# A four-block transformer kernel: SiLU from exponential and logarithm in chunks, and GpSimd's layer norms and bias sum spread over slots

## The chip, the cores and the metric

One core of a Trainium2 chip runs the program. The metric is the device time of one execution, in microseconds (us); lower is better. The kernel is written as five instruction queues, one for each engine: PE (TensorE, matrix products), DVE (VectorE), ACT (ScalarE), POOL (GpSimd) and SP (SyncE, which issues all transfers). Each queue runs in its own order, and the queues meet only at semaphores.

## The reference

The input x is 8 batches of 512 tokens of width 128. Four blocks follow each other, each on the layer norm of x and added to x:

```
x = x + attn_a(layernorm(x))     # 16 heads of width 8, causal, ALiBi slope 1, biases
x = x + ffn(layernorm(x))
x = x + attn_b(layernorm(x))     # full 512x512 scores -> importance of tokens -> 51 picked keys
                                 # + 64 compressed keys; attention over those 115
x = x + ffn(layernorm(x))

ffn(x):  gate = x @ wg.T ; up = x @ wu.T          # wg, wu: 384 x 128, dequantised from int
         return (silu(gate) * up) @ wd.T          # silu(g) = g * sigmoid(g)
layernorm(x) = (x - mean) / sqrt(var + 1e-5)
```

Everything is float32; scores use stacks of bfloat16 parts that together carry float32.

## The kernel before, in words

The work of a batch is written as a list of **slots**. In each slot every engine does the few instructions that it has there, and then goes to the next slot. The counter of a batch is called `a` in the code (its own slots run from -44 to 246), and batch b starts 64 slots after batch b-1, so that four to five batches are in work at once. Slots have no fixed length: a slot is as long as the slowest queue makes it. There are 739 slots in all.

What lies where in a batch's own count:
- -41 to -30: first layer norm, q, k and v of attention A (the P_ constants, lines 423 to 430).
- 0 to 24: first pass over the causal scores, two score tiles a slot, from which VectorE takes the row maxima (`causal_scores` line 1153, `causal_maxima` line 912). 32 to 56: second pass, where ScalarE takes exponentials (line 798) and TensorE weighs the values (`weigh`, line 1189).
- 61 to 74: output projection, residual, layer norm, and the first feed-forward block. I call it **block A**: A_GATE 66, 67, 68; A_SILU 69; A_UP 70, 71, 72; A_DOWN 74.
- 75 to 84: layer norm and projections of attention B. 96 to 160: its **main tiles**, one 128x512 tile of scores a slot.
- 164 to 224: choosing tokens, attention over 115 keys. 226 to 245: projection, residual, layer norm, and the second feed-forward block, **block S**: S_GATE 235, 236, 237; S_SILU 238; S_UP 240, 241, 242; S_DOWN 243.

Modulo 64, block A of batch b lies beside the first causal pass of batch b+1 (slots 2 to 10 of it), and block S of batch b beside the second causal pass of batch b+3 (slots 43 to 51 of it). Both lie beside main tiles of attention B of some batch, except at the ends of the program.

A main tile goes through four engines: TensorE writes its scores into one of three banks (line 1223, one slot ahead); VectorE takes the maximum of each row (`nmB`, line 1045); ScalarE the exponential (line 811) and the logarithm of the sum (line 814); GpSimd a threshold (`thr`, line 680); VectorE, one slot later and at the end of its slot, an entropy sum (`entropy`, line 951, instruction at line 955), which frees the bank.

The order of VectorE in a slot g is: maximum of main tile g; the causal row maxima of the two score tiles that TensorE made in slot g-1; the batch's own steps, among them `hidden` (line 946); the entropy sum of main tile g-1. The order of TensorE in a slot is: scores of main tile g+1; own steps, among them `into_seven` (line 1269), which makes the gate and up products; column sums (`influence`); causal scores. The order of ScalarE is: exponentials of the causal tiles (second pass); main tile; own steps. GpSimd: `thr` of main tile g, then own steps.

The feed-forward block has three chunks c of 128 hidden rows. All products of it, gate and up, go through one bank, bank 7, and `claim` (line 1134) makes TensorE wait until the last user of the bank has been read. Before the change ScalarE copies each gate chunk out in the same slot (line 840, helper line 727). In slot SILU ScalarE runs Silu over all three chunks at once, 128x1536 (line 785), which stands between two loads of the function table (one is recorded at line 785, one at line 786), as all its other functions are in one other table. VectorE multiplies each up chunk from bank 7 by the gate in the slot after it was made (`hidden`). So from `up` to `hidden` to the next `up` TensorE and VectorE take turns.

GpSimd's layer norm `ln` (line 641) does in one slot: variance plus epsilon, the power -1/2, and four 128x128 normalisations (line 652). It lies one slot after VectorE's statistics; TensorE transposes the result (line 1144) two slots later. The sum of x and the output bias, four additions of 128x128 (line 704), lies in slot XBO = 19.

## Time and profile before

| | |
|---|---|
| three timed runs | 1942.92, 1942.50, 1940.46 us; median 1942.5 us |
| the profiled execution | 1941.34 us |
| its span | 1939.2 us, 26667 instructions |
| mean granted clock of TensorE | 0.687 of full speed |
| busy | PE 1524.0 us (79%), DVE 1224.2 us (63%), ACT 1006.8 us (52%), POOL 385.6 us (20%) |
| main tiles | maxima from 245.3 to 1789.5 us of the span, one of 512 in each slot |

The span is that of the profiled execution, and 2.1 us of its time lie around it. A share of busy time is a mean over the program. What sets the length of a slot is found by looking at the instructions of that slot: which queue has no idle time in it, and for whom the others wait. The start of the `nmB` maximum (line 1045) is used as the mark of a slot, since there is just one in each.

### The profile page before, as it was taken

How to read it: one execution, taken by the hardware profiler on the slowest of the kernel's cores; microseconds unless marked ns; L12 is line 12 of the kernel's file. 1: busy time of each engine (PE TensorE's matmuls, PEld its weight loads, DVE VectorE, ACT ScalarE, POOL GpSimd, SP SyncE). 2: the span in 40 equal slices, each digit the busy share in tenths (PEclk: the TensorE clock that was granted, in tenths of full speed). 3: DMA queues.
4: the chain of work that ended last, by engine and by line, in shares of the span. 5: the costliest groups of instructions: out<-in, count | busy, mean ns of one | idle time of the engine just before them, and what ended most of it. 6: DMA issues, size and time to landing. Idle time of an engine off the chain costs nothing.

```text
span 1939.2 us, 26667 instructions
## 1 busy us (share of the span) xinstructions
PE 1524.0 (79%) x8717; PEld 690.2 (36%) x8717; DVE 1224.2 (63%) x3259; ACT 1006.8 (52%) x2542; POOL 385.6 (20%) x900
## 2 busy tenths in 40 slices
PE   1687787878788888898889888788888878678655
PEld 1333443343344343353334343344334332321312
DVE  1503568866976577756876587757786667787211
ACT  1052276466556655656556655665565757546122
POOL 3110311320133011410133022310221012110100
PEclk9555588667766677668667786777666867665555
DMA  2110111121012110112012110221011002100000
GB/s 59 31 36 17 44 52 17 37 60 23 19 41 60 23 22 14 47 44 44 3 49 52 23 24 12 73 36 27 13 35 34 12 8 49 28 13 12 15 10 6
DMA packets 65626, 59.28 MB, mean 31 GB/s; under 512 B 11936, under 2 KB 63184, under 8 KB 65488
## 3 DMA queue, kind: packets, MB, share of 16 engines
q1 hardware_dynamic: 65488, 57.58, 13.3%
q8 instruction: 69, 1.13, 0.3%
q14 instruction: 69, 0.57, 0.1%
HBM read 39.10 MB, written 18.27 MB: 30 GB/s over the span
## 4 chain that ended last, share of the span: by engine, by line
PE 50%; DVE 23%; ACT 13%; issue 6%; POOL 5%; DMA 1%; ACTq 0%; SPq 0%; POOLq 0%; DVEq 0%
PE bank L1231 7%; PE bank L1271 7%; DVE nm L916 6%; DVE junk L955 5%; ACT setup L811 4%; PE bank L1223 4%; PE bank L1199 3%; PE bank L1254 3%; PE bank L1181 3%; PE bank L1159 3%; ACT pT L798 3%; DVE nmB L1045 3%; POOL xn L652 3%; DVE nm L923 2%; PE bank L1390 2%
## 5 line engine op out<-in xcount | busy, mean ns | idle before, releaser
L811 ACT ACTIVATE setup<-bank,nmB 128x512 f32<-128x512 f32 x512 | 350.3, 684 | 291.7 <-DVE nmB L1045 291.6
L955 DVE SCALAR_TENSOR_TENSOR junk<-bank,thr,setup 128x512 f32<-128x512 f32 x512 | 379.4, 741 | 84.8 <-POOL thr L680 81.5
L1045 DVE TENSOR_REDUCE nmB<-bank 128x1 f32<-128x512 f32 x512 | 351.2, 686 | 97.5 <-PE bank L1223 97.0
L1223 PE MATMUL bank<-k_stacks,q_stacks 48*128 48x512 bf16 x512 | 248.6, 487 | 135.5 <-DVE junk L955 133.1
L680 POOL TENSOR_TENSOR thr<-lnZ,nmB 128x1 f32<-128x1 f32 x512 | 96.5, 189 | 1223.5 <-ACT lnZ L814 1223.2
L916 DVE TENSOR_REDUCE nm<-bank 128x1 f32<-128x512 f32 (+3 forms) x512 | 223.7, 483 | 141.4 <-PE bank L1164 138.8
L798 ACT ACTIVATE pT<-bank 128x512 f32<-128x512 f32 (+1 forms) x384 | 184.1, 520 | 174.4 <-PE bank L1185 172.1
L1159 PE MATMUL bank<-k_stacks,q_stacks 52*128 52x512 bf16 (+3 forms) x512 | 177.1, 393 | 38.7 <-DMA k_stacks<-part_dram 17.7
L1231 PE MATMUL bank<-setup,rz 128*1 128x512 f32 x1024 | 196.6, 852 | 0.0
L1181 PE MATMUL bank<-q_stacks,k_stacks 55*128 55x384 bf16 (+3 forms) x512 | 159.2, 359 | 38.3 <-ACT pT L798 32.8
L1223 PEld LDWEIGHTS bank<-k_stacks,q_stacks 48*128 48x128 bf16 x512 | 49.5, 97 | 321.7 <-DVE junk L955 247.4
L1159 PEld LDWEIGHTS bank<-k_stacks,q_stacks 52*128 52x128 bf16 x512 | 54.5, 107 | 189.0 <-issue 121.8
L893 ACT ACTIVATE p<-bank 115x512 f32<-115x512 f32 x128 | 75.3, 588 | 87.3 <-PE bank L1390 87.0
L1199 PE MATMUL bank<-pT,vA 128*9 128x512 f32 (+3 forms) x1024 | 115.0, 554 | 1.0 <-ACT pT L798 1.0
L1162 PE MATMUL bank<-maskr,maskw 64*128 64x64 bf16 x512 | 114.6, 232 | 0.0
L1390 PE MATMUL bank<-s_stacks,kcst 51*115 51x512 bf16 x128 | 75.5, 590 | 49.4 <-ACT p L893 19.5
L814 ACT ACTIVATE lnZ<-Z 128x1 f32<-128x1 f32 x512 | 103.9, 203 | 16.2
L1164 PE MATMUL bank<-maskr,maskw 64*128 64x64 bf16 x512 | 109.0, 219 | 0.0
L1271 PE MATMUL bank<-xnT,wuT 128*128 128x512 f32 x96 | 81.8, 947 | 31.6 <-DVE gated L949 30.3
L1181 PEld LDWEIGHTS bank<-q_stacks,k_stacks 55*128 55x128 bf16 x512 | 52.7, 103 | 145.4 <-issue 81.5
L1183 PE MATMUL bank<-maskr,maskw 64*128 64x64 bf16 x512 | 104.2, 218 | 0.0
L811 ACT ACTIVATION_READ_ACCUMULATOR setup<-bank,nmB 128x1 f32 x512 | 102.2, 200 | 0.0
(193 smaller groups left out, 2437.4 us busy)
## 6 DMA issues: line engine op xcount, KB each, us to landing
part_dram<-part SPq DMA_DIRECT2D x16, 768.0 KB, 3.2
q_stacks<-part_dram SPq DMA_DIRECT2D x192, 64.0 KB
k_stacks<-part_dram SPq DMA_DIRECT2D x192, 64.0 KB
s_stacks<-part_dram SPq DMA_DIRECT2D x48, 128.0 KB
x<-in_L_attn_a_x_dram SPq DMA_DIRECT2D x8, 256.0 KB, 3.2
x_dram<-x SPq DMA_DIRECT2D x8, 256.0 KB, 2.2
x<-x_dram SPq DMA_DIRECT2D x8, 256.0 KB, 2.9
out_dram<-x SPq DMA_DIRECT2D x8, 256.0 KB, 2.2
```

Of the source, the lines that this page charges most:

```text
L798: act.activation(pT[h % HPQ][:, c * T:c * T + WIDTH[c]], bank[3 + u % 2][:, 0:WIDTH[c]], ACT.Exp).then_inc(s_free[3 + u % 2], 1)
L811: act.activation(E[:, n % NE, :], RING[n % RN][:, :], ACT.Exp, bias=nmB[mb % 2][:, h, t:t + 1], accum_out=Z[mb % 2][:, h, t:t + 1]).then_i ...
L916: last = dve.tensor_reduce(nm[0][:, t, h:h + 1], bank[k][:, at:at + (t + 1) * P], AX_X, ALU.max, negate=True)
L955: dve.scalar_tensor_tensor(out=junk[:, :], in0=RING[n % RN][:, :], scalar=thr[mb % 2][:, h, t:t + 1], in1=E[:, n % NE, :], op0=ALU.max, op ...
L1045: dve.tensor_reduce(nmB[mb % 2][:, h, t:t + 1], RING[n % RN][:, :], AX_X, ALU.max, negate=True).then_inc(s_bm, 1)
L1159: pe.matmul(bank[k][:, at:at + (t + 1) * P], qst[0][0:A_SC, h, t * P:(t + 1) * P], kst[0][0:A_SC, h, 0:(t + 1) * P], start=True, stop=True)
L1162: pe.matmul(bank[k][:, at + t * P:at + t * P + HF], maskw[:, 2, :], maskr[:, 2, :], start=False, stop=True, skip_group_check=True)
L1181: pe.matmul(bank[k][:, at:at + w], kst[0][0:A_MX, h, j * P:(j + 1) * P], qst[0][0:A_MX, h, j * P:T], start=True, stop=True)
L1199: last = pe.matmul(bank[5][QROWS * j:QROWS * j + HD + 1, k * P:T], vA[:, k, HPQ * g + j, :], pT[j][:, c * T + at:c * T + at + T - k * P], ...
L1223: pe.matmul(RING[n % RN][:, :], qst[1][0:B_SC, h, t * P:(t + 1) * P], kst[1][0:B_SC, h, :], start=True, stop=True).then_inc(s_bs, 1)
L1231: last = pe.matmul(INFL[QROWS * t:QROWS * t + 1, :], rz[mb % 2][:, h, t:t + 1], E[:, (NT * h + t) % NE, :], start=(h == 0), stop=(h == H - 1))
L1271: pe.matmul(bank[7][:, :], w, xnT[u][:, :], start=True, stop=True).then_inc(s_full[7], 1)
```

## The change

Two edits. First, Silu is replaced. VectorE takes each gate chunk out of bank 7, one slot after it was made, with a maximum against -85 (`gate`). ScalarE makes exp(-g) of it two slots after (`minus_gate`), and three slots after ln(1 + exp(-g)) and exp(-that), which is sigmoid(g) (`sigmoid`), in a new buffer `sigm`. GpSimd multiplies gate and sigmoid four slots after. Exponential and logarithm share one table, so no table is loaded. `hidden` then waits for its own chunk only. Second, GpSimd's layer norm is cut in three: the inverse root in the slot of the statistics, and two normalisations in each of the next two slots; the bias sum is cut into two slots.

```diff
@@ gpsimd
-                def ln(u, b):
+                def inverse_root(u, b):
                     pool.wait_ge(s_mv[u], b + 1)
                     pool.tensor_tensor(ve[u][:, :], mv[u][:, :, 1], eps[:, :], ALU.add).then_inc(s_ve[u], 1)
                     pool.wait_ge(s_ve[u], b + 1)
                     pool.tensor_tensor(rstd[u][:, :], ve[u][:, :], neghalf[:, :], ALU.pow).then_inc(s_rs[u], 1)
+
+                def normalise(u, b, half):
                     pool.wait_ge(s_rs[u], b + 1)
...
-                    for t in range(NT):
+                    for t in (2 * half, 2 * half + 1):
...
-                            if a == LN_AT[u]:
-                                ln(u, b)
+                            if a == STATS[u]:
+                                inverse_root(u, b)
+                            for half in range(2):
+                                if a == STATS[u] + 1 + half:
+                                    normalise(u, b, half)
...
+                        for k in range(2):
+                            for c in range(FC):
+                                if a == GATE[k][c] + 4:
+                                    pool.wait_ge(s_sg[k], FC * b + c + 1)
+                                    pool.wait_ge(s_free[7], turn[7]["gate", k, c, b] + 1)
+                                    pool.tensor_tensor(gated[:, c, :], gated[:, c, :], sigm[:, c, :], ALU.mult
+                                                       ).then_inc(s_sil[k], 1)
+                        for half in range(2):
+                            if a == XBO + half:
...
@@ scalar
-                def silu(k, b):
-                    act.wait_ge(s_free[7], turn[7]["gate", k, FC - 1, b] + 1)
-                    act.activation(gated[:, :, :], gated[:, :, :], ACT.Silu).then_inc(s_sil[k], 1)
-                    act.preload_act_table_set("natural_log_exp_and_others")
+                def minus_gate(k, c, b):
+                    act.wait_ge(s_free[7], turn[7]["gate", k, c, b] + 1)
+                    act.activation(sigm[:, c, :], gated[:, c, :], ACT.Exp, scale=-1.0).then_inc(s_eg[k], 1)
+
+                def sigmoid(k, c, b):
+
+                    act.wait_ge(s_eg[k], FC * b + c + 1)
+                    act.activation(sigm[:, c, :], sigm[:, c, :], ACT.Ln, bias=onesf[:, 0:1]).then_inc(s_lg[k], 1)
+                    act.wait_ge(s_lg[k], FC * b + c + 1)
+                    act.activation(sigm[:, c, :], sigm[:, c, :], ACT.Exp, scale=-1.0).then_inc(s_sg[k], 1)
...
-                                if a == GATE[k][c]:
-                                    out_of(7, ("gate", k, c, b), gated[:, c, :], bank[7][:, :])
-                            if a == SILU[k]:
-                                silu(k, b)
+                                if a == GATE[k][c] + 2:
+                                    minus_gate(k, c, b)
+                                if a == GATE[k][c] + 3:
+                                    sigmoid(k, c, b)
@@ vector
-                    dve.wait_ge(s_sil[k], b + 1)
+                    dve.wait_ge(s_sil[k], FC * b + c + 1)
...
+                def gate(k, c, b):
+
+                    dve.wait_ge(s_full[7], turn[7]["gate", k, c, b] + 1)
+                    dve.tensor_scalar(gated[:, c, :], bank[7][:, :], -85.0, None, ALU.max).then_inc(s_free[7], 1)
...
+                                if a == GATE[k][c] + 1:
+                                    gate(k, c, b)
                                 if a == UP[k][c] + 1:
                                     hidden(k, c, b)
@@ tensor
-                    pe.wait_ge(s_xn[u], b + 1)
+                    pe.wait_ge(s_xn[u], 2 * (b + 1))
```

The waits for `s_xbo` count two steps a batch instead of one. Nothing else changes.

## Rows read from the trace of the kernel before

**Rows 1.** The page's chain of waits that ended last, shares of the span by engine.
```profile
PE 50%; DVE 23%; ACT 13%; issue 6%; POOL 5%; DMA 1%; ACTq 0%; SPq 0%; POOLq 0%; DVEq 0%
```
**Rows 2.** Groups of instructions by line: busy us, mean ns, idle before and its releaser.
```profile
L955 DVE SCALAR_TENSOR_TENSOR junk<-bank,thr,setup 128x512 f32<-128x512 f32 x512 | 379.4, 741 | 84.8 <-POOL thr L680 81.5 <-issue 0.5
...
L652 POOL TENSOR_SCALAR xn<-x,mv,rstd 128x128 f32<-128x128 f32 x128 | 100.8, 799 | 3.3
...
L658 POOL TENSOR_TENSOR rest<-qf,part 128x512 f32<-128x512 f32 x32 | 37.0, 1157 | 20.8 <-ACT part L753 20.8
...
L949 DVE TENSOR_TENSOR gated<-bank,gated 128x512 f32<-128x512 f32 x48 | 32.8, 682 | 50.1 <-ACT gated L785 30.2 <-PE bank L1271 19.9
...
L727 ACT ACTIVATE gated<-bank 128x512 f32<-128x512 f32 x48 | 28.3, 589 | 44.4 <-PE bank L1271 44.4
...
L785 ACT ACTIVATE gated<-gated 128x1536 f32<-128x1536 f32 x16 | 23.7, 1482 | 0.2
...
L785 ACT ACT_TABLE_LOAD x16 | 20.5, 1283 | 0.3
...
L757 ACT ACTIVATE part<-rest 128x512 bf16<-128x512 f32 x32 | 19.8, 620 | 1.5 <-POOL rest L658 1.5
```
**Rows 3.** Three stretches: length; busy PE, PEld, DVE, ACT, POOL; PE clock; DMA share; GB/s.
```profile
946.08:953.14 7.06, 6.43 (x45) 2.48 (x43) 7.06 (x21) 4.74 (x13) 1.66 (x4) 1.00 0.06 14
955.40:967.39 11.99, 8.64 (x34) 2.31 (x32) 9.21 (x22) 6.35 (x16) 0.76 (x4) 0.62 0.01 3
...
885.77:891.86 6.09, 2.38 (x14) 1.31 (x15) 1.54 (x5) 6.02 (x11) 0.19 (x1) 0.85 0.30 44
```
**Rows 4.** Timeline of VectorE, block A of batch 4: start us, length us, what, idle before.
```profile
955.40 0.68 DVE L1045 TENSOR_REDUCE nmB<-bank 128x1 f32<-128x512 f32 x1
...
958.83 0.69 DVE L1045 TENSOR_REDUCE nmB<-bank 128x1 f32<-128x512 f32 x1
960.32 1.23 DVE L916 TENSOR_REDUCE nm<-bank 128x1 f32<-128x256 f32 x2 [0.80 <-PE bank L1164]
...
962.79 0.69 DVE L1045 TENSOR_REDUCE nmB<-bank 128x1 f32<-128x512 f32 x1
...
967.39 0.68 DVE L1045 TENSOR_REDUCE nmB<-bank 128x1 f32<-128x512 f32 x1
```
**Rows 5.** Timeline of TensorE in the same block: a gate product and two up products.
```profile
946.53 1.12 PE L1271 MATMUL bank<-xnT,wgT 128*128 128x512 f32 x2
...
957.99 1.86 PE L1271 MATMUL bank<-xnT,wuT 128*128 128x512 f32 x2 [2.07 <-DVE gated L949]
...
962.26 2.08 PE L1271 MATMUL bank<-xnT,wuT 128*128 128x512 f32 x2 [1.18 <-DVE gated L949]
```
**Rows 6.** Timeline of ScalarE around the SiLU of block S, batch 1.
```profile
882.74 1.09 ACT L798 ACTIVATE pT<-bank 128x512 f32<-128x512 f32 x2 [0.57 <-PE bank L1185]
...
884.74 1.28 ACT L785 ACT_TABLE_LOAD   x1
...
888.83 1.08 ACT L798 ACTIVATE pT<-bank 128x512 f32<-128x512 f32 x2
...
893.48 0.70 ACT L798 ACTIVATE pT<-bank 128x256 f32<-128x256 f32 x2 [0.79 <-PE bank L1185]
```
**Rows 7.** Timeline of TensorE around the same SiLU.
```profile
889.48 0.33 PE L1181 MATMUL bank<-q_stacks,k_stacks 55*128 55x384 bf16 x1 [3.80 <-ACT pT L798]
...
895.99 1.52 PE L1271 MATMUL bank<-xnT,wuT 128*128 128x512 f32 x2
```
**Rows 8.** Timeline of TensorE, block A of batch 0, before the first main tile.
```profile
187.35 2.07 PE L1271 MATMUL bank<-xnT,wuT 128*128 128x512 f32 x2 [1.45 <-DVE gated L949]
```
**Rows 9.** Timeline of VectorE, block A of batch 7, with no causal pass beside it.
```profile
1584.53 0.75 DVE L955 SCALAR_TENSOR_TENSOR junk<-bank,thr,setup 128x512 f32<-128x512 f32 x1 [1.90 <-POOL thr L680]
```
**Rows 10.** Timeline of VectorE, block S of batch 7, at the end of the program.
```profile
1924.95 0.69 DVE L949 TENSOR_TENSOR gated<-bank,gated 128x512 f32<-128x512 f32 x1 [17.66 <-ACT gated L785]
```
**Rows 11.** Who waited for the layer norm's output xn: us in total, times.
```profile
  PE bank L1144: 44.1, 18
```

More of the change, by code:

```diff
@@ L132, in hybrid_block @@
         gated = sb("gated", [P, FC, T])
+        sigm = sb("sigm", [P, FC, T])
         ktok = [sb(f"ktok{s}", [P, 2, NT, P]) for s in range(2)]
@@ L229, in hybrid_block @@
         s_rzo = [sem(f"sums_inverted{s}") for s in range(2)]
+        s_eg = [sem(f"gate_exponentials{s}") for s in range(2)]
+        s_lg = [sem(f"gate_logarithms{s}") for s in range(2)]
+        s_sg = [sem(f"gate_sigmoids{s}") for s in range(2)]
         s_sil = [sem(f"silu_done{s}") for s in range(2)]
@@ L447, in hybrid_block @@
         F_STATS = 75
-        F_LN = 76
         F_LNT = 78
@@ L481, in hybrid_block @@
         SLOTS = FIRST + NMAIN * (B - 1) + S_STORE + 2
-        GATE, SILU, UP, DOWN = (A_GATE, S_GATE), (A_SILU, S_SILU), (A_UP, S_UP), (A_DOWN, S_DOWN)
-        STATS, LN_AT, LN_TURN = (P_STATS, A_PROJ + 1, F_STATS, S_PROJ + 1), (P_LN, A_LN, F_LN, S_LN), (
-            P_TURN, A_LNT, F_LNT, S_LNT)
+        GATE, UP, DOWN = (A_GATE, S_GATE), (A_UP, S_UP), (A_DOWN, S_DOWN)
+        STATS, LN_TURN = (P_STATS, A_PROJ + 1, F_STATS, S_PROJ + 1), (P_TURN, A_LNT, F_LNT, S_LNT)
         LN_BANK = (4, 7, 7, 7)
@@ L578, in _ @@
                             if b:
-                                sp.wait_ge(s_xbo, b)
+                                sp.wait_ge(s_xbo, 2 * b)
                             sp.dma_start(xs0[:, :, :], x[b].rearrange("(t p) d -> p t d", p=P)).then_inc(s_xin, DMA)
@@ L645, in ln @@
                     pool.tensor_tensor(rstd[u][:, :], ve[u][:, :], neghalf[:, :], ALU.pow).then_inc(s_rs[u], 1)
+                def normalise(u, b, half):
                     pool.wait_ge(s_rs[u], b + 1)
-                    if (u, b) in norm_before:
+                    if half == 0 and (u, b) in norm_before:
                         v, other = norm_before[u, b]
                         pool.wait_ge(s_full[LN_BANK[v]], turn[LN_BANK[v]]["ln", v, other] + 1)
-                    for t in range(NT):
+                    for t in (2 * half, 2 * half + 1):
                         last = pool.tensor_scalar(xn[:, t, :], xs[u][:, t, :], mv[u][:, t, 0:1], rstd[u][:, t:t + 1],
@@ L698, in _ @@
                                                    ALU.mult).then_inc(s_sq, 1)
-                        if a == XBO:
-                            pool.wait_ge(s_xin, DMA * (b + 1))
-                            if b:
-                                pool.wait_ge(s_x2st, DMA * b)
-                            for t in range(NT):
-                                last = pool.tensor_tensor(xs1[:, t, :], xs0[:, t, :], bo[:, :], ALU.add)
-                            last.then_inc(s_xbo, 1)
+                        for k in range(2):
[7 more added lines that the diff above has]
+                            if a == XBO + half:
+                                if half == 0:
+                                    pool.wait_ge(s_xin, DMA * (b + 1))
+                                    if b:
+                                        pool.wait_ge(s_x2st, DMA * b)
+                                for t in (2 * half, 2 * half + 1):
+                                    last = pool.tensor_tensor(xs1[:, t, :], xs0[:, t, :], bo[:, :], ALU.add)
+                                last.then_inc(s_xbo, 1)
                         if a == A_TMAX + 1:
@@ L1065, in _ @@
                         if a == A_PROJ + 1:
-                            dve.wait_ge(s_xbo, b + 1)
+                            dve.wait_ge(s_xbo, 2 * (b + 1))
                             residual(xs1, ("proj", 0, b))
```

5 lines of the change are left out of this document (removed).

## The prediction

> **What bounds the kernel now.** I read the shares of busy time first, and they settle nothing: no engine is full over the span. The chain that ended last [rows 1] passes from TensorE to VectorE to ScalarE and has only 5% on GpSimd: a kernel of stages with different limits. So I looked at the slots that the change touches, one block A and one block S, and asked in each which queue has no idle time. In block A, the three slots behind the gate products last 7.06 us together and VectorE is busy for 7.06 us of them (first row of [rows 3]): VectorE is the limit there, TensorE runs beside it at its full clock (1.00, 2.4 GHz), and ScalarE has 2.3 us to spare. In block S of batch 1 the stretch with the SiLU is 6.09 us long; ScalarE is busy 6.02 us of it, TensorE 2.38 us (third row of [rows 3]). There ScalarE is the limit. The same instruction, taken out, is worth different things in the two places.
>
> **The cost of the SiLU now.** A table load takes 1.28 us, the Silu over 128x1536 1.48 us [rows 2], and there are two loads: 4.05 us by the durations, 4.09 us from the first load to the next exponential (888.83 - 884.74, [rows 6]). Over 16 blocks that is 65 us of ScalarE, but only what someone waits for counts. The Trainium skill's page ScalarE: Activation LUTs (section What ACT_TABLE_LOAD costs) says that a switch costs about 2.66 us, a drain of 1.38 us being added to the load. By that each block would give back some 2.7 us more, estimated from the page, and the sum below, with five exposed blocks, would be 14 us lower. In the rows the next instruction follows the load at once, so the measured 4.09 us stands.
>
> **Block S, batches 0 to 4** (second causal pass and main tiles beside it). Removed: the 4.09 us and three copies of 0.59 us [rows 2], 5.9 us of ScalarE. Added: nine passes over 128x512; the nearest row is a conversion from SBUF to SBUF of that size, 0.62 us (line 757, [rows 2]); nine make 5.6 us. So ScalarE does nearly as much as before, only in smaller pieces: 0.6 us in slot 237, 1.9 us in 238 and 239, 1.2 us in 240. Each of these slots also has two causal exponentials (1.09 us [rows 6]) and a main tile, together 2.0 us from 882.74 to 884.74. From 882.74, three slots then take 3.9 + 3.9 + 3.2 = 11.0 us, and the causal exponentials of the slot behind them would start at 893.8 instead of 893.48 [rows 6]. ScalarE as such gains nothing. What is gained is on TensorE: it idled 3.80 us in one piece [rows 7], and its second up product came at 895.99 [rows 7]. With the causal exponentials of each slot no longer behind one long block, I place that product between 892.6 and 894.7, depending on whether TensorE is at its full or half clock: 1.3 to 3.3 us earlier. I take 2, times 5: **-10 us**; bounds 0 (ScalarE full) and -3.8 each. Block S of batch 5 has no causal pass and gains 0.5; in the last two, with nothing beside, `hidden` waited for the Silu until 1924.95 [rows 10], while the first chunk would be ready before its up product; the copy by VectorE costs 0.1 more than ScalarE's, so 0.3 each. Together **-11 us**.
>
> VectorE's copy in block S is covered: VectorE idles most of those slots (busy 1.54 of 6.09 us [rows 3]). Behind it waits the entropy sum, late by up to 0.7 us, which frees a score bank that TensorE wants a slot later; I count nothing.
>
> **Block A, batches 1 to 6** (first causal pass and main tiles beside it). The Silu is hidden here: the up products wait for `hidden` [rows 5], and of the 30.2 us for which `hidden` ever waited for a Silu [rows 2], 17.66 lie in the very last block [rows 10]. So nothing comes back. What is added lies on the full engine: three copies out of bank 7 on VectorE. The nearest row is `hidden`, the same size out of the same bank: 0.68 us, some 0.60 when the next one overlaps it [rows 2]. And the copy brings a new wait. ScalarE emptied bank 7 in the slot in which TensorE filled it; VectorE does it one slot later, behind its main maximum and its causal maxima. TensorE's queue has the next gate product in front of the causal scores of that slot, so it stops at `claim` until VectorE is through, and VectorE then waits for causal scores that come after the product. This turn-taking is in the trace already, in the up slots: TensorE waits 2.07 and 1.18 us for `hidden` [rows 5], the causal maxima wait 0.80 us for TensorE [rows 4], and the slots behind the up products last 3.43, 3.96 and 4.60 us (starts 955.40, 958.83, 962.79, 967.39 [rows 4]), where those behind the gate products last 7.06 / 3 = 2.35 us. The granted clock falls as well, from 1.00 to 0.62 over that stretch [rows 3], so a product takes 2.08 us (1.2 GHz) instead of 1.12 us (2.4 GHz) [rows 5].
> With the change the first gate slot only gets the copy, 2.35 + 0.60 = 2.95 us; the second and third are built like the second and third up slot, 3.96 and 4.60 us. Sum 11.5 us against 7.06: +4.4 us a block, times 6: **+26 us**. Bounds: 3 x 0.60 = 1.8 us if TensorE were never late, 7 us if in addition the half clock stretches the two slots behind by a product's excess of 1 us each. A value near the up slots is right because the code is the same, step for step.
>
> **Block A of batch 0** has no main tiles beside it. TensorE waits 1.45 us in the up slots [rows 8]; twice that for the second and third gate product: **+3 us**. **Block A of batch 7** has no causal pass. There Silu is exposed: the entropy sum waits 1.90 us for a threshold that is late behind it [rows 9]. Spread over slots most of that goes, less the new copies: **-1 us**, bounds -3 and +1.
>
> **GpSimd.** The multiplication costs 1.16 us a chunk (nearest row, line 658, two inputs of 128x512 [rows 2]); 48 of them are 56 us of an engine that is 20% busy. Each stands behind the threshold of its slot and before the next one, in slots of 2.3 us and more; nothing on the path. In block A `hidden` follows only one slot later: threshold, then 1.16 us, and by my count the first chunk is ready 0.2 us before VectorE gets to it. Were it late, some tenths a block would be added, inside the bounds. If that cover were gone, the price would be 1.16 us a block in A. The root now waits for VectorE's statistics in their own slot; behind it on GpSimd stands only the threshold of the next slot, which needs a later maximum of VectorE. The split of the layer norm takes a piece of 4 x 0.80 = 3.2 us (line 652, [rows 2]) plus 1.2 us for the root off the way of thresholds. VectorE's waits for thresholds sum to 81.5 us [rows 2], but nearly all of it is the plain latency through ScalarE. The other place is TensorE's wait for xn, 44.1 us in 18 pieces [rows 11], most of it in the start and the end, where the chain root, four normalisations, transposition is as long as before. I take **-2 us** for both, bounds 0 and -5. The bias sum ends a slot later. Its readers are the residual 42 slots on, and on SP's queue the load of the next x, which so starts about a slot later (2.35 us by the slots above, more in others) and is wanted three slots after that: 0. No transfer is added, and what stands behind that load on SP is issued two slots on.
>
> **Sum.** 26 + 3 - 1 - 11 - 2 = +15 us on the profiled execution's 1941.3 us: 1956.3 us. The median of the three runs is 1.2 us above that execution, so I say 1957 us.
>
> **Rivals.**
> *The gain in block S outweighs (faster).* Place: the 3.80 us idle of TensorE in five blocks S, and the half clock after it (0.85 over that stretch [rows 3]). If all of the 3.8 us came back, 19 us, plus the exposed Silu of batch 7 (3 us) and 5 us from the layer norm, against turn-taking at full clock in block A, 3 us x 6 = 18 and 2 for batch 0: -7 us, 1935. It decides if block A costs under 2.5 us each. For it: ScalarE is plainly the limit in the row of 6.09 us. Against: ScalarE's work there shrinks by 0.3 us only. Chance 0.17.
> *A draw.* The same terms in the middle, block A at 2.5 and block S at -3: 1942 us. Chance 0.10.
> *The half clock spreads.* TensorE idles in the gate slots, its granted clock falls to 1.2 GHz there and stays so up to the up products: 7 us a block in A, nothing gained in S: 42 + 3 - 2 = +43, 1985 us. For it: the clock of 0.62 in the up slots. Chance 0.13.
> That the second edit does nothing (all layer-norm slots as long as before) is possible in each of these cases and moves the time by 2 us only. My forecast has the remaining 0.60.
>
> **How the numbers follow.** About 0.2% (4 us) is about what a measurement of this kernel can tell from no change. Slower by more than that: 0.60 + 0.13 = 0.73; within it: 0.10; faster: 0.17. The range goes from 1936 (the faster rival without its last microseconds) to 1978 (the bounds of block A without the worst).
>
> **What would show it.** Right: slots behind the gate products in blocks A of 1 to 6 grow from 7.06 us to 10 to 12 us, with TensorE idle before the second and third gate product, released by VectorE's copy; the stretch of block S around the old Silu has no TensorE idle piece over 2 us and the second up product comes earlier; ScalarE's nine passes take 0.6 us each; no table load but the first. Wrong: gate slots in block A under 9 us, or blocks S shorter by more than 3 us each, or layer-norm slots that shorten by over 1 us in every period.

## The result, and the profile after

| | before | after |
|---|---|---|
| median of four runs each, same chip | 1942.0 us (1940.5 to 1942.9) | 1967.0 us (1963.2 to 1970.2) |
| the profiled execution, its span | 1941.3, 1939.2 us | 1970.2, 1968.5 us |
| mean granted clock | 0.687 | 0.669 |

The ratio is 1.0125, 95% interval 1.0098 to 1.0153: slower by 25 us. In a second comparison (`e8_after_again`, below) it is 1.0149.

The page of after, shares of busy time, and the chain that ended last by engine:
```profile
PE 1549.8 (79%) x8717; PEld 697.8 (35%) x8717; DVE 1255.9 (64%) x3307; ACT 1002.5 (51%) x2590; POOL 446.9 (23%) x948
...
PE 53%; DVE 24%; ACT 10%; issue 7%; POOL 4%; DMA 1%; SPq 0%; ACTq 0%; DVEq 0%; POOLq 0%
```
VectorE has 32 us more to do, GpSimd 61, ScalarE 4 less. In the chain [rows 1] ScalarE's share went from 13% to 10% and TensorE's from 50% to 53%: the program waits less for ScalarE, and more for TensorE.

Groups by line of after (columns as in [rows 2]; L971 is VectorE's new copy, L966 `hidden`, L796, L801 and L803 the three passes, L706 GpSimd's product, L368 the only table load):
```profile
L1295 PE MATMUL bank<-xnT,wgT 128*128 128x512 f32 x96 | 81.1, 939 | 29.1 <-DVE gated L971 27.8 <-ACT xnT L738 0.7 <-DVE vcat L1033 0.6
L1295 PE MATMUL bank<-xnT,wuT 128*128 128x512 f32 x96 | 79.6, 923 | 31.0 <-DVE gated L966 29.3 <-DVE gated L971 1.6
...
L706 POOL TENSOR_TENSOR gated<-gated,sigm 128x512 f32<-128x512 f32 x48 | 60.9, 1269 | 29.6 <-ACT sigm L803 29.6
...
L801 ACT ACTIVATE sigm<-sigm,onesf 128x512 f32<-128x512 f32 x48 | 34.0, 708 | 0.3
L971 DVE TENSOR_SCALAR gated<-bank 128x512 f32<-128x512 f32 x48 | 32.8, 683 | 28.7 <-PE bank L1295 28.6
L966 DVE TENSOR_TENSOR gated<-bank,gated 128x512 f32<-128x512 f32 x48 | 32.8, 682 | 24.9 <-PE bank L1295 22.7 <-POOL gated L706 2.2
L803 ACT ACTIVATE sigm<-sigm 128x512 f32<-128x512 f32 x48 | 30.2, 630 | 1.5
L796 ACT ACTIVATE sigm<-gated 128x512 f32<-128x512 f32 x48 | 29.6, 616 | 18.4 <-DVE gated L971 18.4
...
L368 ACT ACT_TABLE_LOAD x1 | 1.3, 1283 | 0.8 <-PEq L1458 0.8
```
The gate product of before:
```profile
L1271 PE MATMUL bank<-xnT,wgT 128*128 128x512 f32 x96 | 66.7, 782 | 6.3 <-ACT gated L727 5.0 <-ACT xnT L727 0.7 <-DVE vcat L1011 0.6
```
Its idle time rose from 6.3 to 29.1 us, and VectorE's copy ends nearly all of it. Its mean duration rose from 782 to 939 ns: more of the gate products run at TensorE's lower clock. They now look like the up products beside them (923 ns, 31.0 us).

**Block A of batch 4, the gate slots.** Stretches of after, columns as in [rows 3]; the first is the three slots behind the gate products, the second the four behind them, with the up products:
```profile
961.88:974.02 12.14, 8.83 (x39) 2.77 (x38) 9.17 (x22) 5.22 (x13) 1.67 (x4) 0.58 0.04 9
...
974.02:987.18 13.16, 9.74 (x53) 3.32 (x51) 11.29 (x28) 7.90 (x19) 4.42 (x7) 0.76 0.01 1
```
7.06 us at full clock with a full VectorE [rows 3] became 12.14 us at 0.58, with VectorE idle for 3 us. The timelines of TensorE and VectorE in after:
```profile
960.50 1.12 PE L1295 MATMUL bank<-xnT,wgT 128*128 128x512 f32 x2
964.21 2.07 PE L1295 MATMUL bank<-xnT,wgT 128*128 128x512 f32 x2 [1.80 <-DVE gated L971]
969.08 2.07 PE L1295 MATMUL bank<-xnT,wgT 128*128 128x512 f32 x2 [1.51 <-DVE gated L971]
```
```profile
961.88 0.69 DVE L1067 TENSOR_REDUCE nmB<-bank 128x1 f32<-128x512 f32 x1
962.48 1.07 DVE L933 TENSOR_REDUCE nm<-bank 128x1 f32<-128x128 f32 x3
963.48 0.68 DVE L971 TENSOR_SCALAR gated<-bank 128x512 f32<-128x512 f32 x1
...
964.74 0.68 DVE L1067 TENSOR_REDUCE nmB<-bank 128x1 f32<-128x512 f32 x1
966.96 1.40 DVE L933 TENSOR_REDUCE nm<-bank 128x1 f32<-128x512 f32 x3 [1.54 <-PE bank L1188]
...
968.36 0.66 DVE L971 TENSOR_SCALAR gated<-bank 128x512 f32<-128x512 f32 x1
```
TensorE's first product is ready at 961.6; VectorE does its main and causal maxima first and copies at 963.48; the second product starts at 964.21, at the lower clock; the causal scores come behind it, so VectorE's next causal maxima wait 1.54 us. In the slot behind, the same happens again (TensorE waits 1.51 us for the copy).

**Block S of batch 1.** ScalarE in after, around the sigmoid passes, and the stretch that answers to the 6.09 us of [rows 3]:
```profile
903.27 0.69 ACT L828 ACTIVATE setup<-bank,nmB 128x512 f32<-128x512 f32 x1
...
904.20 0.71 ACT L801 ACTIVATE sigm<-sigm,onesf 128x512 f32<-128x512 f32 x1
904.93 0.63 ACT L803 ACTIVATE sigm<-sigm 128x512 f32<-128x512 f32 x1
905.47 0.61 ACT L796 ACTIVATE sigm<-gated 128x512 f32<-128x512 f32 x1
905.99 1.06 ACT L815 ACTIVATE pT<-bank 128x512 f32<-128x512 f32 x2
```
```profile
905.34:909.01 3.67, 2.14 (x15) 0.95 (x15) 1.54 (x7) 3.61 (x9) 0.97 (x2) 1.00 0.22 50
```
The slot went from 6.09 to 3.67 us, and ScalarE still fills it (3.61 us). TensorE's longest idle piece there is 1.37 us, where 3.80 stood [rows 7]. The second up product of this block in after:
```profile
913.57 2.07 PE L1295 MATMUL bank<-xnT,wuT 128*128 128x512 f32 x2
```
Counted from the start of slot 46 (899.84 us in after, 880.27 us in before) it comes after 13.73 us, where it came after 15.72 us (895.99 [rows 7]).

**The whole program by stretches.** I subtracted the starts of the main maxima (line 1045, after line 1067) between two traces, slot by slot, and summed over the 8 periods. Differences to the profiled execution of before, in us; slots modulo 64. "S gate" are slots 41 to 47, "S SiLU" 48 to 50, "behind S" 51 to 57, "tail" is from the last main tile on:

| | start | A gate (3 to 5) | rest of A | S gate | S SiLU | behind S | other | tail | sum |
|---|---|---|---|---|---|---|---|---|---|
| after | 2.1 | 31.5 | -0.8 | 9.4 | -13.7 | 0.2 | -1.2 | 1.8 | 29.3 |
| e8_after_again | 0.9 | 30.3 | -0.5 | 6.9 | -13.7 | 2.6 | -5.2 | 0.2 | 21.5 |
| e1_act_copy | 0.4 | 0.0 | -0.3 | 4.5 | -12.3 | 2.5 | -6.2 | 1.3 | -10.3 |
| e12_copy_s | -0.9 | 0.2 | 0.0 | 9.6 | -13.3 | 2.7 | -6.2 | -0.3 | -8.2 |
| e13_copy_a | 1.9 | 30.5 | 5.2 | 12.0 | -13.1 | -0.3 | 1.3 | 1.5 | 38.9 |
| e4_copy_first | 1.2 | 11.4 | 5.7 | 5.3 | -14.5 | 2.6 | -3.6 | 0.5 | 8.6 |
| e9_norms_whole | -1.7 | 2.2 | 1.5 | -3.6 | -13.1 | -0.2 | 10.8 | 1.2 | -3.0 |
| e2_norms_only | 0.0 | 0.5 | 1.4 | 7.8 | -5.3 | -2.5 | -5.0 | 0.0 | -3.0 |
| e5_no_silu | -2.4 | 0.5 | -3.2 | -7.8 | -41.0 | 1.9 | 1.5 | -0.7 | -51.2 |
| e7_one_pass | -0.3 | 2.4 | -0.3 | 3.4 | -35.5 | 0.1 | -0.5 | -0.8 | -31.6 |
| e6_early_s | 0.0 | 0.5 | -0.3 | 32.2 | -28.1 | 2.5 | 0.6 | 1.6 | 8.9 |
| e10_spread_s | -1.7 | 0.1 | -0.8 | 13.9 | -34.4 | 37.0 | -0.2 | 6.9 | 20.8 |
| e11_up_late | -0.5 | 0.1 | -0.6 | 8.5 | -18.3 | 25.8 | -2.0 | 0.2 | 13.1 |

Each row is one execution. "A gate" and "S SiLU" repeat within 1.2 us in the two executions of after; "S gate" and "other" differ there by 2.5 and 4.0 us; for the 2.5 the section on the hardware shows the reason. Terms of that size in one trace are not read as effects of an edit.

### The profile page after: what moved, and what is told of

Read it like the earlier page. It is cut to its first block, busy times and chain, and to the rows that moved or that the text cites. A ratio compares the mean times of both kernels' runs of the same rounds, so it can differ in the third digit from the quotient of the medians.

```text
span 1968.5 us, 26859 instructions
## 1 busy us (share of the span) xinstructions
PE 1549.8 (79%) x8717; PEld 697.8 (35%) x8717; DVE 1255.9 (64%) x3307; ACT 1002.5 (51%) x2590; POOL 446.9 (23%) x948
## 4 chain that ended last, share of the span: by engine, by line
PE 53%; DVE 24%; ACT 10%; issue 7%; POOL 4%; DMA 1%; SPq 0%; ACTq 0%; DVEq 0%; POOLq 0%
PE bank L1295 8%; PE bank L1255 8%; DVE nm L933 5%; DVE junk L977 5%; PE bank L1247 4%; PE bank L1223 4%; PE bank L1183 3%; PE bank L1278 3%; PE bank L1205 3%; ACT setup L828 3%; DVE nmB L1067 3%; ACT pT L815 3%; DVE nm L940 3%; PE bank L1414 2%; PE bank L1238 2%
## 5 line engine op out<-in xcount | busy, mean ns | idle before, releaser
L1183 PE MATMUL bank<-k_stacks,q_stacks 52*128 52x512 bf16 (+3 forms) x512 | 185.7, 409 | 37.7 <-DMA k_stacks<-part_dram 17.3
L1255 PE MATMUL bank<-setup,rz 128*1 128x512 f32 x1024 | 205.3, 888 | 0.0
L1186 PE MATMUL bank<-maskr,maskw 64*128 64x64 bf16 x512 | 118.7, 239 | 0.0
L1188 PE MATMUL bank<-maskr,maskw 64*128 64x64 bf16 x512 | 112.4, 224 | 0.0
L1295 PE MATMUL bank<-xnT,wuT 128*128 128x512 f32 x96 | 79.6, 923 | 31.0 <-DVE gated L966 29.3
L1295 PE MATMUL bank<-xnT,wgT 128*128 128x512 f32 x96 | 81.1, 939 | 29.1 <-DVE gated L971 27.8
L1207 PE MATMUL bank<-maskr,maskw 64*128 64x64 bf16 x512 | 103.6, 218 | 0.0
```

Source lines behind the costliest of these rows:

```text
L1183: pe.matmul(bank[k][:, at:at + (t + 1) * P], qst[0][0:A_SC, h, t * P:(t + 1) * P], kst[0][0:A_SC, h, 0:(t + 1) * P], start=True, stop=True)
L1186: pe.matmul(bank[k][:, at + t * P:at + t * P + HF], maskw[:, 2, :], maskr[:, 2, :], start=False, stop=True, skip_group_check=True)
L1255: last = pe.matmul(INFL[QROWS * t:QROWS * t + 1, :], rz[mb % 2][:, h, t:t + 1], E[:, (NT * h + t) % NE, :], start=(h == 0), stop=(h == H - 1))
L1295: pe.matmul(bank[7][:, :], w, xnT[u][:, :], start=True, stop=True).then_inc(s_full[7], 1)
```

## The experiments

Ratios are to the kernel before on the same chip, with the 95% interval. All but `e2_norms_only` and `e5_no_silu` start from after.

**Who copies.** `e1_act_copy` gives the copy back to ScalarE, in the slot of the product:
```diff
@@ scalar, after's kernel
+                                if a == GATE[k][c]:
+                                    out_of(7, ("gate", k, c, b), gated[:, c, :], bank[7][:, :])
@@ vector
-                                if a == GATE[k][c] + 1:
-                                    gate(k, c, b)
```


> The changed kernel, but ScalarE copies each gate chunk out of bank 7 in the slot in which TensorE made it, as before the change; VectorE's copy is gone, everything else of the change stays (no clamp at -85, which these inputs do not need). Theory A (the loss is the turn-taking of TensorE and VectorE at bank 7): the three slots behind the gate products in blocks A fall from 12.1 us back to 7.1 us (31 us over the program), batch 0 gives back 2 us more, the gate slots of blocks S 2 us each, and the 2.4 us gained at the old Silu in each block S stay: about 1925 us, 0.99 of the kernel before. Theory B (the loss comes from GpSimd's multiplication, the later `hidden`, or ScalarE's nine passes): the gate slots fall but the slots of the up products grow, and the time stays over 1955 us.

Measured: 1935.5 us, ratio 0.9984 (0.9971 to 0.9997). The gate slots of block A are as before (0.0 in the table), so VectorE's copy is the whole of their 31 us, and not the product on GpSimd or the smaller passes: theory A holds there. The rest of the change is worth 3 us in this form, well below the 14 us that theory A expected of it.

`e8_after_again` is after, unchanged.

> The changed kernel again, on this chip beside the others, so that e1 and e4 can be held against it: all theories expect 1960 to 1970 us, 1.010 to 1.015 of the kernel before.

Measured: 1963.4 us, ratio 1.0149 (1.0104 to 1.0194).

**Order or length.** `e4_copy_first` keeps the copy on VectorE but places it ahead of the causal maxima:
```diff
@@ vector, after's kernel: behind the main maximum
+                        for k in range(2):
+                            for c in range(FC):
+                                if a == GATE[k][c] + 1:
+                                    gate(k, c, b)
+                    for b, a in now:
...
-                                if a == GATE[k][c] + 1:
-                                    gate(k, c, b)
```


> The changed kernel with one thing moved: VectorE's copy of the gate chunk stands in front of its causal row maxima, behind its main maximum, in the same slot. Theory A (TensorE waits for the copy, which waits behind the maxima): TensorE's idle pieces before the second and third gate product shrink from some 2 us to under 1, and the three slots of blocks A go from 12.1 us to 9 us, so about 1948 us in all. Theory B (it is VectorE's 0.6 us of added work and the half clock, not the order): slots stay at 11.5 us or more, 1963 to 1967 us.

Measured: 1944.5 us, ratio 1.0033 (1.0021 to 1.0046), near theory A's 1948. The gate slots of block A in batch 4, and TensorE's waits there:
```profile
947.27:956.12 8.85, 6.49 (x45) 2.45 (x43) 8.85 (x24) 4.50 (x12) 1.67 (x4) 1.00 0.06 13
```
```profile
948.61 1.12 PE L1298 MATMUL bank<-xnT,wgT 128*128 128x512 f32 x2 [0.81 <-DVE gated L971]
951.47 1.12 PE L1298 MATMUL bank<-xnT,wgT 128*128 128x512 f32 x2 [0.81 <-DVE gated L971]
```
8.85 us with VectorE busy for all of it, at full clock: 7.06 plus three copies of 0.60. TensorE still waits 0.81 us for each copy, but VectorE never waits for TensorE, so only the length counts. Of the 5.1 us of after's gate slots 1.8 are length, and 3.3 are order, the lower clock among them.

**Splitting the copy by block.** `e12_copy_s` keeps VectorE's copy in block S alone, `e13_copy_a` in block A alone (the condition is `k == 0` in the second kernel's vector part, with ScalarE's copy under `k == 1`, and the other way round in the first):
```diff
@@ e12_copy_s, from after's kernel
+                                if k == 0 and a == GATE[k][c]:
+                                    out_of(7, ("gate", k, c, b), gated[:, c, :], bank[7][:, :])
...
-                                if a == GATE[k][c] + 1:
+                                if k == 1 and a == GATE[k][c] + 1:
                                     gate(k, c, b)
```


> After, but ScalarE copies the gate chunks out of bank 7 in block A as before; only block S keeps VectorE's copy. This prices the term that the prediction counted as nothing. Theory that the copy in block S is covered: the time of e1_act_copy, ratio 0.998 to 0.999. Theory that it costs about 0.4 us a block by its length and up to 6 us over all through slots 42 to 45 (the difference of after and e1_act_copy there in the profiled executions): ratio 1.000 to 1.002. In both theories the three slots behind the gate products of block A stay at 7.06 us.

> The complement: after, but ScalarE copies the gate chunks in block S as before; only block A keeps VectorE's copy. If the two copies add up, e12_copy_s and e13_copy_a lie above e1_act_copy by parts that sum to the 1.5% between e1_act_copy and after. Theory that block A is all of it: ratio 1.013 to 1.015, as after. Theory that block S has a share of 6 us: ratio 1.009 to 1.012. The three slots behind the gate products of block A take about 12 us as in after.

Measured: `e12_copy_s` 1928.9 us, ratio 0.9947 (0.9933 to 0.9960); `e13_copy_a` 1979.8 us, ratio 1.0196 (1.0174 to 1.0217). Both theories of the first expectation missed: VectorE's copy in block S is neither free nor a cost, it gains 0.4% against `e1_act_copy`, and 0.5% to 0.7% if after and its repeat are held against `e13_copy_a`. So `e12_copy_s` is the fastest version here that still computes the SiLU, 10 us faster than before. The copy in block A costs more than either theory of the second expectation said: 2.1% of time (`e13_copy_a` against `e1_act_copy`), or 1.8% (after against `e12_copy_s`): 35 to 41 us. The two parts, -0.4% and +2.1%, add up to the 1.4% to 1.7% between `e1_act_copy` and after. The table finds 31 us of block A's loss in the three gate slots. For block S's gain I looked at the last two blocks S, which stand in the tail. `hidden` in `e1_act_copy`, then in `e12_copy_s`:
```profile
L968 DVE TENSOR_TENSOR gated<-bank,gated 128x512 f32<-128x512 f32 x48 | 32.8, 682 | 49.3 <-POOL gated L706 31.2 <-PE bank L1295 18.0
```
```profile
L968 DVE TENSOR_TENSOR gated<-bank,gated 128x512 f32<-128x512 f32 x48 | 32.8, 683 | 25.5 <-PE bank L1297 23.3 <-POOL gated L706 2.2
```
With ScalarE copying, its queue has the third copy ahead of the first chunk's logarithm and second exponential, and `hidden` waits for the product on GpSimd; with VectorE copying it doesn't. But 28.7 of the 31.2 us stand in the last two blocks S, where VectorE has little else to do, and most of that wait is idle time that costs nothing. From the first gate product of batch 7 to its second up product `e12_copy_s` takes 11.44 us and `e1_act_copy` 11.70: 0.26 us are gained. Of the 1.6 us by which the table's tail is shorter, 1.0 lies ahead of the first gate product of batch 6, where after and its repeat differ by 0.8 as well. So no trace shows where the 7 us between these two kernels lie: their profiled executions differ by 2 us in the other direction, each being off its median (1930.6 against 1935.5 us, and 1932.7 against 1928.9 us). The runs of `e12_copy_s` had a mean granted clock of 0.687 to 0.692, those of `e1_act_copy` 0.683 to 0.690, so TensorE's clock is a rival to the copy itself that I can't exclude.

**What the SiLU holds.** `e5_no_silu` is before with no SiLU and no table loads; the product with up uses the gate as it is:
```diff
@@ scalar, before's kernel
-                    act.activation(gated[:, :, :], gated[:, :, :], ACT.Silu).then_inc(s_sil[k], 1)
-                    act.preload_act_table_set("natural_log_exp_and_others")
+                    act.activation(gated[:, :, 0:1], gated[:, :, 0:1], ACT.Copy).then_inc(s_sil[k], 1)
```


> The kernel before without Silu and without its two table loads (the gate goes into the product as it is; a copy of three columns keeps the semaphore). It prices the Silu block: what can be won at most by taking it away. Theory A: nothing in blocks A 1 to 6, 3 us in block A of batch 7, 3.5 us in each of six blocks S: 1918 us. Theory B (it is exposed in every block): 16 times 4 us, 1880 us. Theory C (ScalarE's other work fills the place): under 2.4 us a block S, over 1925 us.

Measured: 1898.6 us, ratio 0.9806 (0.9756 to 0.9856). It lies between theory A (1918) and theory B (1880): the blocks S give back nearly 7 us each in the table, twice what A said. `e7_one_pass` is `e1_act_copy` without the logarithm and the second exponential; the gate is multiplied by exp(-g):
```diff
@@ scalar, e1_act_copy's kernel
-                    act.activation(sigm[:, c, :], sigm[:, c, :], ACT.Ln, bias=onesf[:, 0:1]).then_inc(s_lg[k], 1)
-                    act.wait_ge(s_lg[k], FC * b + c + 1)
-                    act.activation(sigm[:, c, :], sigm[:, c, :], ACT.Exp, scale=-1.0).then_inc(s_sg[k], 1)
+                    act.activation(sigm[:, c, 0:1], sigm[:, c, 0:1], ACT.Copy).then_inc(s_sg[k], 1)
```


> The kernel e1_act_copy without the logarithm and the second exponential (a copy of one column keeps the semaphore; GpSimd still multiplies), so the gate is multiplied by exp(-g) and not by the sigmoid. Theory A (six passes of 0.6 us in ScalarE's full slots of block S are what keeps the gain at 2 us): the slot that held the Silu is 4 us shorter than before, the one behind it 2.4 us, as without Silu at all: about 1905 us. Theory B (it is GpSimd or the up products): unchanged from e1, 1935 us.

Measured: 1910.1 us, ratio 0.9829 (0.9795 to 0.9863), as theory A said within 5 us. The slot of the SiLU in block S of batch 1, in `e5_no_silu` and in `e7_one_pass`:
```profile
870.10:872.07 1.97, 1.97 (x16) 0.85 (x14) 1.54 (x7) 1.94 (x7) 0.19 (x1) 1.00 0.14 45
```
```profile
876.00:878.48 2.48, 2.14 (x15) 0.95 (x15) 1.54 (x5) 2.45 (x9) 0.97 (x2) 1.00 0.13 38
```
6.09 us [rows 3], 3.67 in after, 2.48 with one pass of three, 1.97 with none. ScalarE is busy for all but 0.06 us of each: this slot is as long as ScalarE's work in it, and in `e5_no_silu` TensorE is full too. The whole SiLU is worth 38 us by the timed runs (1.94% of 1938.5); in the traces its slots in block S shrink by 41.0 us. The change got 13.7 of these back, `e7_one_pass` 35.5. So the passes hold the rest, and GpSimd's product, which `e7_one_pass` keeps, holds next to nothing.

**Can the passes be moved?** `e6_early_s` takes exp(-g) of block S straight from bank 7 in the slot of the product, and the other two passes one slot after it; ScalarE's copy of a chunk stands behind that exponential:
```diff
@@ scalar, e1_act_copy's kernel, block S (k = 1)
+                    act.activation(sigm[:, c, :], bank[7][:, :] if k else gated[:, c, :], ACT.Exp, scale=-1.0
...
-                                if a == GATE[k][c] + 2:
+                                if a == GATE[k][c] + 2 * (1 - k):
...
-                                if a == GATE[k][c] + 3:
+                                if a == GATE[k][c] + 3 - 2 * k:
```


> The kernel e1_act_copy (ScalarE copies the gate in its own slot) with the passes of blocks S moved two slots forward: exp(-g) straight from bank 7 in the slot of the product, logarithm and second exponential one slot later. Same number of passes, but most of them in slots where TensorE is the limit (ScalarE was idle half of them). Theory A (what the Silu cost in blocks S comes back only as far as ScalarE's passes leave the slots of the second causal pass that ScalarE limits): the two slots around the old Silu, which e1 shortened by 2.0 us a block, shorten by some 5 us, the gate slots grow by under 1 us: 10 to 15 us less than e1, 0.990 to 0.993 of the kernel before. Theory B (the rest of the 6.5 us belongs to GpSimd's multiplication or the clock): as e1, 0.998.

Measured: 1949.6 us, ratio 1.0049 (1.0029 to 1.0069), a miss. The SiLU slots gained 28 us, but the gate slots lost 32. Gate products of `e1_act_copy`, then of `e6_early_s`:
```profile
L1295 PE MATMUL bank<-xnT,wgT 128*128 128x512 f32 x96 | 68.5, 801 | 6.5 <-ACT gated L738 5.0 <-ACT xnT L738 0.7 <-DVE vcat L1035 0.6
```
```profile
L1299 PE MATMUL bank<-xnT,wgT 128*128 128x512 f32 x96 | 75.6, 879 | 11.8 <-ACT gated L738 10.3 <-ACT xnT L738 0.7 <-DVE vcat L1039 0.6
```
ScalarE's copy of the next chunk now stands behind the passes, TensorE waits 5.3 us more for it, and its products are slower (879 against 801 ns, 7.1 us in all). These are 12 of the 28 us by which the gate slots grew against `e1_act_copy`; the rest I did not trace.

`e11_up_late` moves the up and down products of block S and its store five slots later, `e10_spread_s` does so too and gives each pass a slot of its own:
```diff
@@ constants, e1_act_copy's kernel (both)
-        S_UP = (240, 241, 242)
-        S_DOWN = 243
-        S_STORE = 245
+        S_UP = (245, 246, 247)
+        S_DOWN = 248
+        S_STORE = 250
@@ e10_spread_s alone: logarithm, second exponential, GpSimd's product
+                                if a == GATE[k][c] + (3, 5)[k]:
+                                    log_of(k, c, b)
+                                if a == GATE[k][c] + (3, 8)[k]:
...
+                                if a == GATE[k][c] + (4, 9)[k]:
```


> The kernel e1_act_copy with blocks S stretched: up products, down product and store five slots later (S_UP 245 to 247), and ScalarE's nine passes one a slot (exponentials in slots 237 to 239, logarithms 240 to 242, second exponentials 243 to 245, GpSimd's products one slot after each). Theory A (three passes in one slot, 1.9 us, are more than the slot has left beside 2.0 us of other work; one pass, 0.6 us, is not): the slots 46 to 50 (modulo 64) shrink as without Silu, 4 us at 48 and 1 to 2 us at 49, and slots 51 to 56 grow by the up products moved there: 10 to 15 us less than e1, about 0.992 of the kernel before. Theory B (ScalarE's work is on the path whatever its place): as e1, 0.998.

> The kernel e1_act_copy with up products, down product and store of blocks S five slots later, but the passes three a slot as in e1: the control for e10. Theory A: the move itself gives nothing, 0.997 to 1.000 of the kernel before. Theory B (the place of the up products is what counts): the same as e10.

Measured: `e10_spread_s` 1960.7 us, ratio 1.0115 (1.0092 to 1.0138), a miss of both theories; `e11_up_late` 1957.2 us, ratio 1.0114 (1.0087 to 1.0140), the same as `e10_spread_s`, as its theory B said: the place of the up products is what counts. Spreading the passes does what it should (S SiLU -34 against -12 us in `e1_act_copy`). But the later place is no better: behind S the slots grow by 26 to 37 us. One of them, slot 57 of the period shown above, in `e11_up_late` and in `e1_act_copy`:
```profile
905.23:910.35 5.12, 5.12 (x55) 3.38 (x53) 3.05 (x9) 2.05 (x7) 0.19 (x1) 1.00 0.54 104
```
```profile
907.51:909.87 2.36, 2.29 (x25) 0.62 (x17) 2.36 (x8) 1.84 (x7) 0.38 (x2) 1.00 0.52 123
```
The down products of `e11_up_late` run from just before that slot:
```profile
904.70 2.94 PE L1278 MATMUL bank<-wdT,gated 128*128 128x128 f32 x24 [0.30 <-DVE gated L968]
```
These 2.94 us lie where TensorE was full already (2.29 of 2.36 us in `e1_act_copy`), and the slot grows by 2.76.

**The second edit.** `e2_norms_only` is before with the second edit alone; `e9_norms_whole` is `e1_act_copy` without it. Each diff is the GpSimd part of the change without, or with only, the SiLU lines.

> The kernel before with the second edit alone: root, two and two normalisations, and the bias sum in two slots. Theory A: as in the prediction, 2 us less than before, 1940 us, and all gate and Silu slots as before. Theory B (the second half, behind one more threshold, is late for TensorE's transposition and takes part of the loss): 1946 us or more, with longer waits for xn. Theory C (thresholds behind the layer norm matter more than I counted): 1935 us or less.

> The kernel e1_act_copy with the layer norm and the bias sum of GpSimd whole again, each in one slot as before the change. Theory A (the split moves nothing that can be measured): within 3 us of e1, 0.997 to 1.000 of the kernel before. Theory B (the split carries e1's gain): 1.002 or more. Theory C (the split costs): 0.995 or less.

Measured: ratio 1.0006 (0.9980 to 1.0031) and 0.9995 (0.9973 to 1.0016). With `e1_act_copy` at 0.9984 the split is worth nothing that these runs can tell. It moves time about: `e2_norms_only` has slot 1 shorter by 4.1 us over the program (2.1 of it in the first period, 1.4 in the seventh), slot 38 longer by 5.2, and the gate slots of block S longer by 7.8. The last may be TensorE's clock. In the five blocks S that have a causal pass beside them, slot 43 takes either 2.50 to 2.66 us or 3.45 us. In the stretches of slots 43 and 44 shown in the last section the granted clock was 1.00 with the shorter form and 0.50 with the longer. The longer form stands in two of the five in before and in none in `e9_norms_whole` and `e5_no_silu`, the three kernels with the layer norm whole; in the eleven traces with the split it stands in three to five. That is one execution of each kernel (two of after), and not a proof.

## Why the prediction came out as it did

The sign, the mechanism of the loss and the range were right; the size was 10 us short (+25 against +15). By its own steps, against the profiled execution (+28.9 us in time, 29.3 in span):

- **Block A, batches 1 to 6: forecast +26, right in kind.** The forecast said 11.5 us for the three slots behind the gate products; batch 4 has 12.14. Slot by slot they are 2.86, 4.86 and 4.42 us, where the forecast had 2.95, 3.96 and 4.60. The middle one was too short: its causal maxima wait 1.54 us for TensorE, those of the up slot that it was modelled on 0.80 us [rows 4], and they are longer (1.40 against 1.23 us). The up slots behind gave 1.1 us back (13.16 us against 14.25 before, from 953.14 to 967.39 in the trace of before). Over the six blocks the gate slots grew by 30.7 us and the others gave 1.4 back: +29.3 us. The cause, turn-taking at bank 7, is shown by `e1_act_copy` (gone with the copy) and `e4_copy_first` (two thirds gone with the order alone).
- **The bounds.** The lower bound of 1.8 us a block, "if TensorE were never late", is what `e4_copy_first` measured: 8.85 - 7.06 = 1.79.
- **Block A, batch 0: forecast +3, measured +2.1** (start of the first main tile). Batch 7: forecast -1; its nine slots (2 to 10) take 22.9 us instead of 21.9. The entropy sums there no longer wait for thresholds, the 1.90 us of [rows 9] among them. But the gate slots grew by 0.7 us, slot 2 by 0.8 (1.0 in `e2_norms_only`, which has no copy: the layer norm's work came there from slot 1, 1.4 us shorter), and `hidden` waits 2.15 us for the product on GpSimd where it waited 1.16 us for the Silu.
- **Block S, forecast -11: the part at the SiLU was right, the gate slots were not in it.** In slots 48 to 50 the five blocks with a causal pass gave -9.7 us, forecast -10, and the second up product of batch 1 comes 2.0 us earlier, the 2 us that were forecast. Some luck is in the sum: slot 48 gave 2.4 us in each of them, but slots 49 and 50 gave between +1.2 and -0.8. Batch 5, forecast -0.5, gave -3.7: the SiLU was exposed there too. Together with a small rest -13.7 us. But slots 41 to 47 grew by 9.4 us (6.9 in the repeat), which the prediction had at nothing, so that the whole gave -4.3. Of the 9.4, 2.5 lie in a period that has no block S, and the rest goes with the clock level: in batch 0, where both traces have the lower level, the seven slots differ by 0.03 us; batch 1 fell by 4.3 us, where only before has the lower level, and batches 2 to 4 grew by 4.2, 3.6 and 3.2, where only after has it. `e2_norms_only`, with no change at the gates, has +7.8 there. So nothing here ties this loss to VectorE's copy.
- **"VectorE's copy in block S: count nothing"** holds in the traces: at one and the same clock level the copy makes slot 44 longer, from 2.81 to 3.28 us in batch 0, and the next one shorter by 0.45. The timed runs say that it gains: `e12_copy_s` is 0.4% below `e1_act_copy`. It takes 0.6 us a chunk off ScalarE, which would fit, but where the 7 us lie is not shown.
- **The size again, by the timed runs.** The change without VectorE's copy in block A, `e12_copy_s`, is 10.3 us below before (0.53%), where the forecast's terms for block S and the layer norm add up to 13. By the timed runs the shortfall is therefore in block A: forecast 26 + 3 - 1 = 28 us, measured 35 to 41. The trace of after has 33 of it at the start and in block A; where the rest lies is open. So the two readings divide the missing 10 us differently: by one execution's trace more of it is the gate slots of block S, that is the clock there, by the differences of medians it is block A.
- **Layer norm, forecast -2: nothing measurable.** That was within its bounds.
- **GpSimd's product, forecast at nothing: right in blocks A 1 to 6,** though it takes 1.27 us and not 1.16. `hidden` waited for it once, 2.2 us, in block A of batch 7.
- **ScalarE's passes, forecast 0.6 us each:** 0.62, 0.71 and 0.63, so 1.96 us a chunk instead of 1.86. The pass with the logarithm is the dearer one; the last section says why that need not be the function.
- **The table load.** With the Silu and both loads gone (`e5_no_silu`) the slot fell from 6.09 to 1.97 us, 4.12 less; the trace's own 4.09 us explains that. By the 2.66 us a switch that the Trainium skill gives (ScalarE: Activation LUTs, What ACT_TABLE_LOAD costs) I estimate 2 x 2.66 + 1.48 = 6.8 us. The measurement decides: the two loads cost their recorded 1.28 us each here.
- **The rivals.** "The gain in S outweighs" needed block A under 2.5 us; `e4_copy_first` has it at 1.8 and is still slower than before by 0.3%. "The half clock spreads" said 7 us a block and nothing in S: the clock did fall in the gate slots (1.00 to 0.58), but it was higher, not lower, in the up slots behind (0.76 against 0.68).

## What to carry to other kernels

An evacuation of a bank that the next product needs must not stand behind work that itself waits for the product's queue: place it first (`e4_copy_first`, 0.3% instead of 1.3% to 1.5%) or on an engine that is free in the same slot (`e1_act_copy`). Decide this stage by stage: the same copy on VectorE costs 35 to 41 us beside the causal maxima and, by the timed runs, gains some 7 us beside the exponentials, and only the version that treats the two blocks differently is clearly faster (0.9947; `e1_act_copy` has 0.9984). Before spreading the work of one engine into later slots, look at what fills those slots: in `e6_early_s`, `e10_spread_s` and `e11_up_late` the gain was there and was given back a few slots away.

## What the runs showed of the hardware

**One piece of code has two lengths with TensorE's clock.** Gate slots 43 and 44 of block S in the kernel before, batch 2 and batch 1, and the same two of after in batch 2:
```profile
1085.18:1089.28 4.10, 3.52 (x32) 1.50 (x32) 2.81 (x6) 3.60 (x12) 0.38 (x2) 1.00 0.00 0
869.59:875.84 6.25, 6.11 (x33) 2.13 (x33) 2.87 (x8) 3.59 (x12) 0.38 (x2) 0.50 0.01 3
```
```profile
1107.30:1114.03 6.73, 6.59 (x33) 2.53 (x34) 3.50 (x9) 4.03 (x14) 0.38 (x2) 0.50 0.00 1
```
At a granted clock of 1.00 (2.4 GHz) the two slots take 4.10 us, at 0.50 (1.2 GHz) 6.25 us. The level of a stretch can differ between executions of the same kernel: slots 43 and 44 of the second period take 4.79 us at 0.50 in after and 4.12 us at 1.00 in `e8_after_again`, and slots 41 to 47 there differ by 2.5 us. In all, `e8_after_again` and after differ by 7.8 us in their sums, with 0 in the SiLU slots and 1.2 in block A's gate slots. All of it lies in the first two periods, the last one, and the start and tail: from the third period to the seventh no slot differs by more than 0.1 us between the two. What picks the level is not shown by these runs.

**Two-input operations on GpSimd depend on more than the size.** Three of them over 128x512 in after, a product of a float32 tile with itself, a subtraction whose second input is bfloat16, and the new product of two float32 tiles (line 706, 1269 ns, shown above):
```profile
L699 POOL TENSOR_TENSOR kw<-ktok 128x512 f32<-128x512 f32 x16 | 16.6, 1039 | 0.0
L657 POOL TENSOR_TENSOR rest<-qf,part 128x512 f32<-128x512 f32 x32 | 37.0, 1155 | 20.7 <-ACT part L764 20.7
```
The operation alone does not explain it, since the two products are 0.23 us apart; no run separates the operands.

**ScalarE's second function in the same table costs nothing to switch to.** No table load stands between exponential and logarithm, and ScalarE was idle for 0.3 us ahead of all 48 logarithms. The logarithm takes 0.71 us, the exponential before it 0.62, both over 128x512 from SBUF to SBUF. But the logarithm here has a bias that it reads from a tile (`bias=onesf[:, 0:1]`), and the exponential has none. Two exponentials in after that read a bank, one with such a bias (line 828, which also sums), one without (line 815):
```profile
L828 ACT ACTIVATE setup<-bank,nmB 128x512 f32<-128x512 f32 x512 | 350.3, 684 | 323.1 <-DVE nmB L1067 323.0
L815 ACT ACTIVATE pT<-bank 128x512 f32<-128x512 f32 x256 | 141.6, 592 | 133.7 <-PE bank L1209 131.6
```
They differ by the same 0.09 us, so the bias operand is the likelier reason; a logarithm without it was not run.
